# Spreading bias rows and gates with TensorE instead of broadcast loads, with five weight and input loads moved and a new instruction order, in a four-layer attention kernel

## What is computed

```
phase 0  x = x + attention(rope(x@Wq+bq), rope(ctx@Wk), ctx@Wv+bv) @ Wo + bo
phases 1,2  (per 128-token half) shift, scale, gate = silu(c) @ ada_w + ada_b
            x = x + gate * (self_attention(norm(x)*(1+scale)+shift) @ proj_w + proj_b)
MLP      x = x + gate3 * (gelu(mod(norm(x)) @ fc1 + b) @ fc2 + b)
phase 3  x = layernorm(x + attention(x, ctx) @ W_o + b_o) * gamma + beta
phase 4  x = x + attention(layernorm(x)*gamma+beta, ctx; ternary weights) @ Wo + bo
```

## Time and profile before

| | us |
|---|---|
| median of 3 runs (lowest, highest) | 299.56 (298.98, 306.13) |
| the profiled execution | 298.25 |
| its span, first to last instruction | 296.4 |
| around the span | 1.85 |
| PE busy | 258.8 (87%) |
| DVE, ACT, POOL busy | 215.8, 215.0, 218.5 |
| mean granted TensorE clock | 0.977 |

### The profile page before, as it was taken

One profiled execution on the slowest core, in us unless ns is written; L12 is line 12 of the kernel. 1 busy time (PEld: TensorE's weight loads), 2 busy tenths in 40 slices (PEclk: granted clock), 3 DMA queues, 4 the chain that ended last, 5 costly groups with the idle time before them and its releaser, 6 DMA issues.

```text
span 296.4 us, 8985 instructions
## 1 busy us (share of the span) xinstructions
PE 258.8 (87%) x3172; PEld 161.9 (55%) x3172; DVE 215.8 (73%) x463; ACT 215.0 (73%) x462; POOL 218.5 (74%) x393
## 2 busy tenths in 40 slices
PE   2837997999996779768899999999999999999995
PEld 2524544555645566545666766656464646455553
DVE  2399997798845636835572788867889999999923
ACT  2133587698887387476769888898979797878992
POOL 6896757467887588897599889898989988882120
PEclk9986999999999799997999999999999999999999
DMA  4569142523346033453113322221123222221002
GB/s 136 165 176 253 49 126 67 137 80 92 104 124 164 5 80 96 138 134 92 31 46 83 91 59 56 59 54 29 47 65 81 56 66 52 73 67 29 4 3 71
DMA packets 41363, 24.74 MB, mean 83 GB/s; under 512 B 4960, under 2 KB 39656, under 8 KB 41320
## 3 DMA queue, kind: packets, MB, share of 16 engines
q1 hardware_dynamic: 37144, 17.71, 23.2%
q10 hardware_dynamic: 3792, 5.41, 6.3%
q0 software_dynamic: 384, 1.05, 1.2%
HBM read 7.56 MB, written 0.54 MB: 27 GB/s over the span
## 4 chain that ended last, share of the span: by engine, by line
PE 54%; DVE 10%; DMA 9%; POOL 8%; ACT 8%; issue 7%; SPq 3%; POOLq 0%; ACTq 0%; DVEq 0%
PE ps L768 11%; PE ps L726 10%; PE ps L725 8%; PE ps L696 7%; DVE neg_max L1042 6%; PE ps L794 5%; DMA q_stack<-max_rows_split 4%; ACT probs L899 4%; PE ps L761 4%; PE ps L856 3%; POOL heads_normed L529 2%; SPq L490 2%; DMA q_stack<-q_parts 2%; PE ps L867 2%; PE ps L804 1%
## 5 line engine op out<-in xcount | busy, mean ns | idle before, releaser
L1042 DVE TENSOR_REDUCE neg_max<-ps 128x2 f32<-128x512 f32 (+1 forms) x256 | 160.4, 682 | 32.1 <-PE ps L725 31.2
L899 ACT ACTIVATE probs<-ps 128x512 f32<-128x512 f32 x256 | 134.5, 608 | 14.7 <-PE ps L726 12.5
L725 PE MATMUL ps<-k_stack,q_stack 62*128 62x256 bf16 (+1 forms) x640 | 63.7, 257 | 10.1 <-DMA q_stack<-q_parts 4.7
L726 PE MATMUL ps<-q_stack,k_stack 64*128 64x256 bf16 (+1 forms) x640 | 59.3, 252 | 6.2 <-DMA q_stack<-max_rows 2.5
L768 PE MATMUL ps<-probs,v_cols 128*32 128x256 f32 x768 | 52.3, 385 | 0.7 <-ACT probs L899 0.6
L725 PEld LDWEIGHTS ps<-k_stack,q_stack 62*128 62x128 bf16 x640 | 31.3, 96 | 32.1 <-issue 10.8
L726 PEld LDWEIGHTS ps<-q_stack,k_stack 64*128 64x128 bf16 x640 | 30.1, 95 | 29.1 <-issue 9.5
L768 PEld LDWEIGHTS ps<-probs,v_cols 128*32 128x32 f32 x768 | 20.2, 109 | 18.2 <-issue 8.1
L518 POOL CAST max_parts<-neg_max 128x16 bf16<-128x16 f32 (+2 forms) x34 | 6.8, 201 | 26.6 <-DVE neg_max L1042 26.2
L933 ACT ACTIVATE q_f<-ps,vec 128x256 f32<-128x256 f32 x32 | 15.1, 479 | 7.1 <-PE ps L794 6.7
L1068 DVE RECIPROCAL inv_sum<-ps 128x32 f32<-128x32 f32 x20 | 7.1, 355 | 18.0 <-PE ps L696 17.9
(11 more groups left out here) (120 smaller groups left out, 425.3 us busy)
## 6 DMA issues: line engine op xcount, KB each, us to landing
k_stack<-k_parts SPq DMA_DIRECT2D x120, 64.0 KB, 2.1
q_stack<-q_parts SPq DMA_DIRECT2D x114, 64.0 KB, 2.1
gates<-gates_dram ACTq DMA_DIRECT2D x4, 384.0 KB, 3.8
w<-in_w ACTq DMA_DIRECT2D x2, 512.0 KB, 4.6
rows<-in_rows ACTq DMA_DIRECT2D x1, 704.0 KB, 6.7
q_stack<-max_rows_split SPq DMA_DIRECT2D x44, 4.0 KB
w<-in_w ACTq DMA_DIRECT2D x1, 576.0 KB, 5.5
ctx_t<-in_ctx_t SPq DMA_DIRECT2D x4, 128.0 KB, 2.9
```

The source lines that it names most:

```text
L725: return nc.tensor.matmul(out, queries, keys, start=True, stop=True)
L726: return nc.tensor.matmul(out, keys, queries, start=True, stop=True)
L899: nc.scalar.activation(probs[:, n % PROB_BUFS, :], ps[bank_of["score", p, b, i]][:, :], ACT.Exp, scale=SCALE).then_inc(of(st), 1)
L1042: nc.vector.tensor_reduce(dst, src, AX.X, ALU.max, negate=True).then_inc(of(st), 1)
```

## The change

- `rows` shrinks to 8 rows. They are loaded once, as 4 KB, into partition 0 of a cleared tile `one_row`, by SP behind batch 1. Two PE steps `bias_rows` multiply it (512 columns each) with column 0 of the identity, broadcast to 128 columns, as the stationary operand; this writes the row to all 128 partitions of a bank. Two ACT steps copy the banks into `rows`.
- The three gate bias rows come as `gate_rows` on 8 partitions (12 KB), by SP.
- `gates_small` becomes 128 partitions, cleared by POOL. The store to HBM and the four broadcast loads go. Instead PE has 8 steps `spread` (384 columns each, float32, column `2b+i` of the identity as selector) and ACT 8 steps `take_spread` that copy 384 columns from PSUM into `gates`.
- POOL gets two memsets ahead of `clear_v` and `preset_stacks` of batch 0: `one_row` (128 x 1024) and `gates_small` (128 x 384).
- `x` and `w` groups 2, 1 and 3 are issued by SP directly behind batch 3, ahead of SP's first placements. Only groups 4 and 5 are left on ACT's queue.
- `ORDER`, `BANK_OF` and `COUPLED` are new (coupled pairs: 190, before 185). Groups 4 and 5 stand at the exponentials of the first unit, right behind `exp` 11 and `exp` 15 of (0, 0). POOL's first steps are the gathers of batches 1, 2 and 3, before the preset of batch 1; PE's first steps are k of batches 0 and 1, then q of batch 0. DVE splits q of batch 0 before k, and both after `turn_k` and `rope_add_k` of batch 1. `bias_rows` stand on PE behind q of batch 2, with the first `max` later; the `spread` steps stand where the table says.
- A second, unreachable copy of the branches `base` and `base_mlp` on POOL is deleted.

| spread step (batch, half) | what stands near it |
|---|---|
| (0,0), (0,1) | phase 0, batch 2's scores |
| (1,0), (1,1) | ahead of the values of (1, 0) |
| (2,0), (2,1) | ahead of the first maxima of (1, 2) |
| (3,0), (3,1) | around the first maxima of (2, 0) and (2, 1) |

```diff
-LOADS = ("x", "rows", 2, 1, 3, 4, 5)
-SPREADS = B
+BIAS_ROWS = 2
+LOADS = (4, 5)
...
-        "4": ("act", only([("keep_gates", 0, 0)] + [("spread", 0, i) for i in range(SPREADS)], first)),
+        "4": ("pe", [("spread", 0, i) for i in range(2)]),
+        "8": ("act", [("take_spread", 0, i) for i in range(2)]),
+        "+": ("pe", only([("bias_rows", 0, i) for i in range(BIAS_ROWS)], first)),
+        "-": ("act", only([("take_bias_rows", 0, i) for i in range(BIAS_ROWS)], first)),
...
             load_batch(sp, 1)
+            sp.wait_ge(one_row_cleared, 1)
+            sp.dma_start(one_row[0:1, :], a["rows"].partition_broadcast(1)).then_inc(rows_loaded, 16)
+            sp.dma_start(gate_rows[:, :, :].rearrange("p r c -> p (r c)"), a["gate_rows"].partition_broadcast(2 * B)
+                         ).then_inc(gate_rows_loaded, 16)
             sp.wait_ge(gathered[0], NT * 16)
             load_batch(sp, 2)
             load_batch(sp, 3)
+            sp.dma_start(x[:, :, :, :].rearrange("p b n c -> p (b n) c"), a["x"].rearrange("b (n p) c -> p (b n) c", p=P)
+                         ).then_inc(x_loaded, 16)
+            for group in (2, 1, 3):
+                load_w(sp, group)
...
+            nc.gpsimd.memset(one_row[:, :], 0.0).then_inc(one_row_cleared, 1)
+            nc.gpsimd.memset(gates_small[:, :, :].rearrange("p k c -> p (k c)"), 0.0).then_inc(gates_cleared, 1)
...
+                elif kind == "spread":
+                    pe.wait_ge(const_loaded, 16)
+                    pe.wait_ge(gates_cleared, 1)
+                    pe.wait_ge(*done("take_gate", 0, 0, 0))
+                    row = 2 * b + i
+                    last = nc.tensor.matmul(out[:, 0:3 * D], ident[:, row:row + 1].broadcast_to([P, P]),
+                                            gates_small[:, :, :].rearrange("p k c -> p (k c)"), start=True, stop=True)
+                elif kind == "bias_rows":
+                    pe.wait_ge(const_loaded, 16)
+                    pe.wait_ge(rows_loaded, 16)
+                    n = len(R_NAMES) * D // BIAS_ROWS
+                    last = nc.tensor.matmul(out[:, 0:n], ident[:, 0:1].broadcast_to([P, P]), one_row[:, n * i:n * (i + 1)],
+                                            start=True, stop=True)
...
-                elif kind == "keep_gates":
-                    act.wait_ge(*done("take_gate", 0, 0, 0))
-                    act.dma_start(gates_dram.rearrange("(r c) -> r c", r=2 * B),
-                                  gates_small[:, :, :].rearrange("r k c -> r (k c)")).then_inc(gates_stored, 16)
...
+                elif kind == "take_spread":
+                    act.wait_ge(*done("spread", p, b, i))
+                    nc.scalar.activation(gates[:, 2 * b + i, :, :].rearrange("p k c -> p (k c)"),
+                                         ps[bank_of["spread", p, b, i]][:, 0:3 * D], ACT.Copy).then_inc(of(st), 1)
```

More of the change, by code:

```diff
@@ new lines @@
+COUPLED = (
+    "0101010000000010100100001000100000100010101010101001000100001010100101010101010101001010101010101010010101010101"
+    "0100001000000001010010100101001010101010010101001000010101010000010010100101000001001010010010101010000101010010"
+    "1000101001010010101001010100101000001010100000010100101010101001010101010001010101010010100000001010101010101000"
+    "0101010010000100101010101010001001001010010101000000101010001010010001010101010000010010100001001010101001010010"
+    "1010101010000010010101001010101010101010101001010010010101010101")
@@ L246, in signal @@
             return own[kind]
-        if kind in ("stack_k", "stack_q", "gather", "load", "keep_gates", "spread"):
+        if kind in ("stack_k", "stack_q", "gather", "load"):
             return None
@@ L334, in build @@
         mods = sb("mods", [P, 6, 2 * B])
[L335 removed]
+        gates_small = sb("gates_small", [P, 3, D])
         gates = sb("gates", [P, 2 * B, 3, D])
@@ L386, in build @@
         max_placed = [[sem(f"max_placed{g}{i}") for i in range(B)] for g in range(4)]
-        gates_stored = sem("gates_stored")
-        gates_spread = [sem(f"gates_spread{i}") for i in range(B)]
+        gate_rows_loaded = sem("gate_rows_loaded")
+        one_row_cleared = sem("one_row_cleared")
+        gates_cleared = sem("gates_cleared")
         out_stored = sem("out_stored")
@@ L902, in _ @@
                     place_parts(act, kind[-1], p, b, i)
[L903 to L908 removed]
                 elif kind == "load":
                     load_w(act, LOADS[i])
[L911 to L920 removed]
+                elif kind == "take_spread":
+                    act.wait_ge(*done("spread", p, b, i))
+                    nc.scalar.activation(gates[:, 2 * b + i, :, :].rearrange("p k c -> p (k c)"),
+                                         ps[bank_of["spread", p, b, i]][:, 0:3 * D], ACT.Copy).then_inc(of(st), 1)
+                elif kind == "take_bias_rows":
+                    act.wait_ge(*done("bias_rows", p, b, i))
+                    n = len(R_NAMES) // BIAS_ROWS
+                    nc.scalar.activation(rows[:, n * i:n * (i + 1), :].rearrange("p r c -> p (r c)"),
+                                         ps[bank_of["bias_rows", p, b, i]][:, :], ACT.Copy).then_inc(of(st), 1)
                 elif kind in ("take_k", "take_q"):
@@ L1108, in _ @@
                     dve.wait_ge(*done("gate", 0, 0, 0))
-                    dve.wait_ge(rows_loaded, 16)
-                    nc.vector.tensor_tensor(gates_small[:, :, :],
+                    dve.wait_ge(gate_rows_loaded, 16)
+                    dve.wait_ge(gates_cleared, 1)
+                    nc.vector.tensor_tensor(gates_small[0:2 * B, :, :],
                                             ps[bank_of["gate", 0, 0, 0]][0:2 * B, 0:3 * D].rearrange("p (a b) -> p a b", a=3),
-                                            rows[0:2 * B, R_AT["gate1"]:R_AT["gate3"] + 1, :], ALU.add).then_inc(of(st), 1)
+                                            gate_rows[:, :, :], ALU.add).then_inc(of(st), 1)
                 elif kind == "quant_abs":
@@ L1169, in host_layout @@
             "vec": np.stack([v[n] for n in V_NAMES], axis=1),
-            "rows": np.concatenate([r[n] for n in R_NAMES])}
+            "rows": np.concatenate([r[n] for n in R_NAMES]),
+            "gate_rows": np.concatenate([r[f"gate{n}"] for n in (1, 2, 3)])}
 def constants():
```

136 lines of the change are left out of this document (51 added, 85 removed).

## The result

The changed kernel takes 304.99 us (median of four runs, 302.21 to 307.07), the kernel before, timed beside it, 299.48. The ratio is 1.0151, with a 95% interval of 1.0090 to 1.0212: slower by 1.5%. The ratio leaves out the slowest execution of each kernel, so it is not the quotient of the medians. The time lies in the forecast range and within 2%, but 298.5 was forecast, no change. The profiled execution took 303.49 us (span 301.4), 5.24 more than that of before.

The account below looks back on a forecast made before the run. PE was taken as the bound where it is fed. Terms -5.2 -1.7 +5.1 +0 +2.5 +0.3 +0.5 -1.5 sum to 0.0, giving 298.25 us profiled or 299.56 from the median; 298.5 was taken, range 291 to 306.

Parts of the forecast that it names:

- step 7: Groups 4 and 5 at about 38 and 43 us: group 4 collides with a maxima placement, +0.5 us (0 to 2).
- step 5: At the start, 1.64 MB of loads ahead of SP's first placements delay the first maxima: +2.5 us (0 to 4.7).
- rival C: At the start, loads on SP's queue hold the first placements, first maxima after about 26 us: 306.5 us, chance 0.15.
- Step 6: At the start, POOL's two new memsets delay the gather of batch 0: +0.3 us (0 to 0.6).
- Step 1: Stalls beside removed loads and gate transfers, at 41.73, 63.05, 94 and 130.99 us, shrink: -5.2 us (2 to 8.8).
- Step 2: Behind the two long stalls, the full-speed work lost to a lower granted clock is half regained: -1.7 us (0 to 3.4).
- Step 3: Eight spreads on PE, two in phase 0 and six between 80 and 140 us: +5.1 us (2 to 6.4).
- Step 4: At the start, bias-row products and copies fall where PE is partly idle: cost 0, without this cover 2.1 us.
- Step 8: The new order, between 30 and 280 us, removes a tenth of PE's other idle time: -1.5 us (-4 to +3).

## Why the prediction was wrong

Placed along the kernel, the forecast and the traces compare so (the last column adds up to the 5.0 us by which the last `add_out` is later):

| stretch | terms of the forecast | forecast | measured |
|---|---|---|---|
| to the first scores | start +2.5, memsets +0.3, bias rows 0 | +2.8 | +6.6 |
| first scores to `add_out` of (0, 1) | stall of 41.73 -1.5, step 7 +0.5 | -1.0 | -0.2 |
| from there to the end | stalls -3.7, clock -1.7, spreads +5.1, order -1.5 | -1.8 | -1.4 |

*What failed is step 5,* "the start": +2.5 was taken, with 4.7 and a first `max` at 27.3 as the far end. It starts at 27.90, so the criterion of the text for its rival C holds (later than 26). Loads alone, on the kernel before, cost 5.0 at the first maxima and 5.6 at the end. Two things in it were wrong.

First, the working took the free share of the DMA engines times 250 GB/s as room for the loads and so came to 2.2 us. But 250 GB/s is no fixed rate of full engines. They moved 344 at 1.03 while the loads ran, and 199 at 1.14 in 22.6:27.9, where placements were being worked off; in the earlier trace rows it was 250 at 0.95. Bytes of placements took more engine time than bytes of loads. And placements don't fit into what is free over 12.6 us: they come behind what is queued when they are issued. With 1.6 MB issued at 13.3 to 16 us, whatever is issued at 16 to 22 lands 5 to 8 us later, and the last one of these decides (21.14, landed 6.67 later). The upper bound, a plain sum in order, was nearest. The sentence that SP's issue itself isn't late was wrong too: the four loads end at 16.05, not 14.1, and the first placement is issued at 16.17. With the loads on ACT's queue it is issued at 14.8 and the first maxima are no earlier (28.3), so this decided nothing.

Second, the text let the delay pass on unchanged to the first scores ("DVE passes the delay on"). It grew by 1.3 us instead. PE had nothing to do for 4.5 us and then ran at 1.2 GHz up to 38 us, while DVE no longer was the bound in that stretch (9.76 of 11.8 us busy, PE 11.80); with the gap filled the stretch was 1.0 shorter. A difference of this size between two traces can also be chance. The rival which ends slower named the place and the threshold, but priced neither this nor the mechanism rightly: 306.5, with a chance of 0.15.

The mechanism of C, that the loads' row holds the placements, is refuted by the loads on ACT's row: 7.0 to 8.9 us from issue to landing on the row without loads, 6.2 to 7.0 on the row with them. The result of C came in another way, most likely by the engines' time. The rule of the Trainium skill quoted in step 5 (DMA: Bandwidth & Descriptors, "Queues, rings and completion order") may hold as it stands; a row of its own just bought nothing here. What packets the two kinds are made of was not measured.

*Step 6,* the memsets: +0.3 was taken (0 to 0.6). The gather starts 1.1 us later, and with the memsets off POOL the first maxima came 0.6 and the end 1.4 earlier, in one trace. The step counted POOL's own time and not that DVE is held meanwhile.

*Step 1,* the stalls: those of 94 and 131 us went, as said. With their two loads alone taken out of the middle, PE's idle time behind (0, 1) fell by 2.5 us, where the step had 1.4 + 2.0 = 3.4. The stall of 41.73, its other 1.5, only moved: PE now waits 1.33 at 51.55.

*Step 2,* the clock, gave nothing: it is 0.94 in 80:140 both before and after, where over 0.97 was announced, and at the end of that stretch it is still low:

```profile
128.00:140.00 12.00, 10.61 (x104) 7.15 (x107) 5.33 (x12) 7.05 (x20) 9.95 (x19) 0.72 0.28 70
```

With groups 4 and 5 early on the kernel before it even cost 1.2 us instead of giving 1.7.

*Step 3,* the spreads: a spread holds PE 0.81 to 0.91 us by itself, a little over the 0.74 to 0.80 of the text, but the work behind it starts after 0.64 to 0.75, so eight take 5.5. The step had 5.1, less than their full 6.0 because the gaps would take a part. The test "step 3 is wrong if the idle time falls by as much as the spreads add" is met: idle time between 80 and 140 fell by 7.5 us. But it is a poor test, since the stalls that went fall into the same stretch; the doubled spreads left the idle time as it was. No run shows that gaps swallowed the spreads, and none prices the eight by taking them out.

*Behind (0, 1) as a whole* PE's idle time fell by 7.1 us, from 21.6 to 14.5, and its busy time grew by 5.7. Stalls and order were to give 5.2, the spreads to take 5.1, the clock to give 1.7. So the sum, -1.8 against -1.4, is near because the idle time fell by more than forecast and the clock gave nothing: in part luck. How the 7.1 divide between stalls, order and spreads was not separated. With the -1.8 and the start as measured, +6.4 at (0, 1), the text would have come to 302.9; the profiled execution took 303.49.

*Step 4* held in the changed kernel, whose first maxima wait for a placement: the bias rows cost nothing where they stand, and 2 us where the cover is gone. With the loads apart it is not quite so; there PE's last wait ahead of the first maxima, 0.99 us, ends with ACT's copy of the bias rows. *Step 7* was too low, and its times were off: groups 4 and 5 are issued at 47.2 and 49.8 us, not at 38 and 43, since all of the start is later, and group 4 collides as group 2 did at 41.73; PE's 1.33 us of waiting stand against the +0.5. *Step 8,* the new order: with loads and memsets put right, the changed kernel is faster than before by 1.3%, but how much of this is the order, and how much the gates' missing transfers, was not separated.

The forecast of an even trade is about what the middle of the kernel shows. The sum missed since the start was priced by the free share of the DMA engines.

## What to carry to other kernels

Before bulk loads are moved into a stretch, ask which small transfer is issued just behind them and who waits for it: here 1.6 MB cost 5 us, and issued apart, between 24 and 57 us, they cost nothing. Count the queue at the moment of issue, not the mean free share of a stretch, and give each kind of transfer its own rate. When PE is going to be idle for several us ahead of work that PE itself bounds, add the work behind it at the lower clock to the price. Read what closing a stall gave as idle time and busy time apart: here 2.5 us of idle time went and 1.4 reached the end, since the clock took the rest. And learn from two traces of the same instructions how far they differ before a difference of 1 or 2 us is explained.

## What the runs showed of the hardware

- A placement (a 64 KB copy inside the chip) took 2.0 to 2.7 us from issue to landing with the DMA engines not full, and 4 to 9 us behind 1.6 MB of loads, on the same queue row or on another.
- Full DMA engines moved 344 GB/s (share 1.03) while loads ran and 199 GB/s (share 1.14) while placements were worked off.
- After 4.5 us without work PE ran at a granted clock of 0.50 from about 26 to 38 us though it was busy from 27.9 on; with eight idle products in the gap the same stretch had 0.84. In the kernel before, after 4.3 us without work, it was 0.50 only from 22 to 26 us and full again from 28.
- DVE's TENSOR_SCALAR of 128 x 8 float32, 0.17 us by itself, took 0.88 beside POOL's memset and ended 0.03 us after it. The CAST ahead of it (0.77) ended 0.02 after the memset before that.
- A float32 product of 384 columns held PE 0.81 us, and an equal one behind it started 0.64 to 0.75 us later; two of 512 columns held it 1.9 at full clock and 4.15 at 1.2 GHz.
